# Recurrence on 28 segments of 112 steps instead of 16 of 196, handled one step at a time

## The chip, the core and the metric

The kernel runs on one core of a Trainium2 chip. A core has five engines with queues of their own: TensorE (PE in the profile; its weight loads are PEld), VectorE (DVE), ScalarE (ACT), GpSimd (POOL) and SyncE (SP), which issues the DMAs here. They are ordered only by semaphores. The metric is the device time of one execution in microseconds, lower is better.

## The reference, cut to what matters

The input is x, (16, 56, 56, 128) in float32: 16 images of T = 3136 tokens with 128 channels. Layer 0 is a shifted window attention after a group norm. Layer 1 is a causal linear attention and then this recurrence, which is where the change is:

```
t  = t + linear_attention(layernorm(t))
z  = layernorm(t) @ W.T
wx = (z - mean) * rsqrt(var + 1e-5) * gamma + beta      # over all 16*3136 tokens
for each of the 3136 tokens of an image, in order, all 16 images side by side:
    y  = sigmoid(wx[token] + y @ V.T)                   # V is orthogonal, y starts at 0
out = t + y of every token
```

## The kernel before

It has three stages, each with the work of all engines laid over one another: window attention (tiles `wa_`), linear attention (`la_`) and the recurrence (`sc_`, function `scan`).

The recurrence is made parallel by cutting each image into SEGS segments of STEPS tokens. All segments of all images run side by side as COLS = 16 x SEGS columns. Every segment but the first needs the state at the end of the one before. It gets it from a warm-up: WARM = 12 steps over the last 12 tokens of every segment, started from 0.5. Their end states are handed one segment on as start states, and then the main pass of STEPS steps runs over all tokens. After it, the true end states are compared with the start states that were used. Only if some pair differs by more than 5e-7 is the main pass run again, SEGS - 1 times.

One step t is worked in two halves h of HALF columns. TensorE issues, in `scan`'s tensor block, `state_part(t, h)` (V times the state of t-1, L1488) and `input_part(t + 1, h)` (W times the next tokens, L1478), h = 0 and then h = 1. Both accumulate in one PSUM bank of the half. In float32 each matmul stands as two instructions in the trace. ScalarE then takes the sigmoid of the half (L1562) into `sc_y`. A half's next L1488 waits for its sigmoid, so each half is a ring PE, ACT, PE, and the two halves take turns on PE.

Around it, work goes in tiles of up to LONGEST = 10 steps (`MAIN_PLAN`). SP loads a tile of tokens from DRAM scratch `t2` into `sc_tb` (4 buffers, L1436). GpSimd multiplies it by the layer-norm scale into `sc_ub` (2 buffers, L1240), two tiles ahead. VectorE transposes it in 32x32 blocks into `sc_uT` (L1503), a pair of steps at a time, three pairs ahead. It also transposes the states back: for the first 3 of 5 pairs of a tile straight into the output tile `sc_ob` (L1523), where GpSimd adds the residual in one instruction (L1463); for the others into PSUM (L1525), from where VectorE adds the residual itself (L1534). SP stores the tile (L1428). SP's queue is in order: the store of tile j-4 stands ahead of the load of tile j. GpSimd's too: the scaling of tile j stands ahead of the residual of tile j-2.

The layout ties the stages. Linear attention works in units of 256 tokens, 196 in all, one per 3.98 us, and stores each token into `t2` at segment and step; each stretch of tokens that lies in one segment is a DMA of its own (`pieces`, L789). The tail of a unit is on SP: load of unit n+4 (L780), stores of unit n-5. The blocks 0 to EARLY_BLOCKS - 1 of 32 columns are complete before the stage ends, so the first three warm-up tiles are loaded for these blocks at unit EARLY_AT (L1229), and GpSimd scales the first two of them four units later (L1240 again, among `la_spread`, `la_rstd` and `la_tn`, L1019, L1025, L1030). The remaining blocks are loaded and scaled when the stage is over. `measure_gap` (L1309) and `compare` (L1326 to L1333) come last.

Of the kernel before, what the change touches and what calls it, by code (L numbers as in the profile page):

```python
# [26 lines left out]
SEGS = 16  # L27
# [3 lines left out]
SQ = 32  # L31
# [1142 lines left out]
class Recurrence:  # L1174
# [13 lines left out]
    def allocate(self, ctx):  # L1188
        nc = self.nc

        def sb(name, shape):
# [12 lines left out]
                          ob=sb("ob", [C, KEPT_TILES, LONGEST, COLS]), uT=sb("uT", [C, U_PAIRS, 2, COLS]), y=sb("y", [C, Y_PAIRS, 2, COLS]))  # L1204
# [168 lines left out]
def scan(nc, block, t2, out, plan, ffn, signals, ident, bank):  # L1373
# [36 lines left out]
    def vector_sums(j):  # L1410

        return sum(plan[i][1] // 2 - by_pool(i) for i in range(FIRST, j))
# [57 lines left out]
    def _(pe):  # L1470
        def input_part(t, h):
# [24 lines left out]
    def _(dve):  # L1496
        def turn_tokens(p):
            if not inside(p, PAIRS):
                return
            j, i = where[p]  # L1500
            dve.wait_ge(u_made, j + 1)
            at_least(dve, w_done, 4 * (p - U_PAIRS + 1))
# [3 lines left out]
        def hand(p):  # L1506
            if p != 1 or not WARMED:
# [6 lines left out]
        def turn_states(p):  # L1514
            if not inside(p, PAIRS) or p < WARM_PAIRS:
                return
            j, i = where[p]
            for h in range(2):
                dve.wait_ge(y_made[h], 2 * p + 2)
            at_least(dve, stored[slot(j)], stores(j))  # L1520
            states = y[:, p % Y_PAIRS].rearrange("p s c -> p (s c)")
            if i < 2 * by_pool(j):
                nc.vector.transpose(ob[:, slot(j), i:i + 2, :].rearrange("p s c -> p (s c)"), states).then_inc(y_turned, 1)  # L1523
            else:
                nc.vector.transpose(b_y[p % 2], states).then_inc(y_turned, 1)  # L1525
# [106 lines left out]
```

## Time and profile before

| | us |
|---|---|
| median of 3 runs | 1782.33 |
| lowest and highest | 1781.41, 1783.42 |
| profiled execution, its own time | 1784.76 |
| profiled execution, span of instructions | 1782.8 |
| window attention | 0 to about 771 |
| linear attention | about 771 to 1568 |
| recurrence | about 1574 to 1774 |

The profiled execution is one execution under the profiler. Its own time is 1.9 us above its span, and 2.4 us above the median of the runs. Stage borders are read from where the stages' instructions start.

### The profile page before, as it was taken

To read this page: it belongs to the slowest core of one execution; us is meant where nothing else is said; L and a number is where in the kernel's file an instruction comes from. 1 tells how busy PE (TensorE), PEld (TensorE's weight loads), DVE (VectorE), ACT (ScalarE), POOL (GpSimd) and SP (SyncE) were. 2 spreads that over 40 slices of the span, in tenths; PEclk is the share of its full clock that TensorE was granted. 3 is DMA by queue.
4 is the path that set the end of the run, shared out by engine and by line. 5 is a ranking of instruction groups with operands and counts; after the bars stand their busy time and mean duration, and the time that the engine had idled before them with its cause. 6 is when DMAs were issued, how large, how long until landed. Compare 5 with 4: busy or idle time off the path is not lost.

```text
span 1782.8 us, 58142 instructions
## 1 busy us (share of the span) xinstructions
PE 1749.7 (98%) x19648; PEld 1587.7 (89%) x19648; DVE 1509.8 (85%) x4546; ACT 1269.8 (71%) x3387; POOL 1073.7 (60%) x1202
## 2 busy tenths in 40 slices
PE   7999999999999999989999999999999999989997
PEld 6888888888888888879999999999999999989997
DVE  7889888888888888778888888888888888868787
ACT  5877778887887788856666666666666666657776
POOL 6887888888888888843333333333333333368874
PEclk9999999999999999999999999999999999999999
DMA  5333343433333332313334434343434443457774
GB/s 167 105 103 104 104 110 99 109 107 102 110 103 104 106 106 70 83 43 70 73 67 68 70 68 70 68 67 68 70 68 70 68 68 70 86 178 277 291 278 176
DMA packets 361816, 188.30 MB, mean 106 GB/s; under 512 B 221760, under 2 KB 348720, under 8 KB 356656
## 3 DMA queue, kind: packets, MB, share of 16 engines
q1 hardware_dynamic: 360368, 183.40, 41.0%
q8 instruction: 164, 2.69, 0.7%
q14 instruction: 132, 1.08, 0.2%
q10 hardware_dynamic: 1152, 1.13, 0.2%
HBM read 106.58 MB, written 77.87 MB: 103 GB/s over the span
## 4 chain that ended last, share of the span: by engine, by line
PE 52%; issue 28%; POOL 17%; DVE 1%; DMA 1%; POOLq 0%; ACT 0%; ACTq 0%; SPq 0%; DVEq 0%
POOL la_rstd L1025 12%; PE k_psum L349 7%; PE k_psum L299 6%; PE k_psum L292 6%; PE k_psum L1488 6%; PE k_psum L317 6%; PE k_psum L333 6%; PE k_psum L365 5%; PE k_psum L1478 5%; PE k_psum L283 5%; POOL la_spread L1019 3%; POOL la_tn L1030 2%; DMA wa_group<-in_group 0%; POOLq L42 0%; DMA t<-la_tn 0%
## 5 line engine op out<-in xcount | busy, mean ns | idle before, releaser
L1019 POOL TENSOR_SCALAR la_spread<-la_mv 128x4 f32<-128x4 f32 (+1 forms) x203 | 46.2, 228 | 476.1 <-DVE la_mv L1130 476.0
L618 POOL TENSOR_TENSOR wa_prob<-wa_prob,wa_peak 128x784 f32<-128x784 f32 x128 | 195.0, 1523 | 116.8 <-DVE wa_peak L484 116.8
L966 ACT ACTIVATE la_ve<-k_psum 128x256 f32<-128x256 f32 x196 | 75.6, 386 | 231.9 <-PE k_psum L847 231.9
L1025 POOL TENSOR_TENSOR la_rstd<-la_spread,k_exponent 128x4 f32<-128x4 f32 (+1 forms) x203 | 207.8, 1024 | 17.2 <-POOL la_spread L1019 0.4
L625 POOL TENSOR_TENSOR wa_prob<-wa_prob,wa_inv 128x784 f32<-128x784 f32 x128 | 195.2, 1525 | 11.3 <-DVE wa_inv L445 11.3
L835 PE MATMUL k_psum<-la_uT,la_wt 128*128 128x256 f32 x784 | 201.9, 380 | 0.0
L1085 DVE SCALAR_TENSOR_TENSOR la_fqk<-k_psum,la_raised 128x512 f32<-128x512 f32 x196 | 135.4, 691 | 72.8 <-ACT la_raised L958 72.6
L1562 ACT ACTIVATE sc_y<-k_psum,sc_cols 128x128 f32<-128x128 f32 x414 | 152.3, 368 | 51.9 <-PE k_psum L1488 8.8
L476 DVE TENSOR_TENSOR wa_prob<-k_psum,wa_bias 128x784 f32<-128x784 f32 x128 | 124.9, 976 | 66.2 <-PE k_psum L317 66.1
L1488 PE MATMUL k_psum<-sc_y,sc_vT 128*128 128x128 f32 x824 | 171.0, 289 | 0.0
L958 ACT ACTIVATE la_raised<-k_psum,la_minus_one 128x512 f32<-128x512 f32 x196 | 134.8, 688 | 43.9 <-PE k_psum L835 43.7
L1478 PE MATMUL k_psum<-sc_uT,sc_fT 128*128 128x128 f32 x832 | 161.7, 276 | 2.8 <-DVE sc_uT L1503 2.8
L525 ACT ACTIVATE wa_kb<-k_psum,wa_own 128x392 f32<-128x392 f32 x256 | 136.5, 584 | 38.2 <-PE k_psum L292 38.2
L544 ACT ACTIVATE wa_vb<-k_psum 49x256 f32<-49x256 f32 x256 | 97.0, 379 | 90.8 <-PE k_psum L299 89.1
L333 PEld LDWEIGHTS k_psum<-k_ident,wa_prob 113*128 113x128 f32 x1024 | 118.2, 142 | 43.5 <-issue 23.7
L886 PE MATMUL k_psum<-la_ve,la_kt 128*128 128x129 f32 (+1 forms) x768 | 150.7, 278 | 1.8 <-ACT la_state L982 1.6
L904 PE MATMUL k_psum<-la_ve,la_aT 128*128 128x129 f32 x784 | 151.7, 276 | 0.0
L908 PE MATMUL k_psum<-la_state,la_fqk 128*128 128x129 f32 (+1 forms) x768 | 148.9, 275 | 0.0
L637 POOL TENSOR_TENSOR wa_xb<-wa_xw,wa_bout 112x384 f32<-112x384 f32 (+1 forms) x128 | 146.9, 1148 | 0.0
L349 PE MATMUL k_psum<-wa_pT,wa_vb 128*64 128x49 f32 x4096 | 146.5, 224 | 0.1
L556 ACT ACTIVATE wa_pT<-k_psum 128x452 f32<-128x452 f32 x256 | 140.2, 548 | 8.4 <-PE k_psum L333 5.3
L349 PEld LDWEIGHTS k_psum<-wa_pT,wa_vb 128*64 128x64 f32 x4096 | 130.0, 138 | 17.8 <-ACT wa_pT L556 0.5
(137 smaller groups left out, 5205.3 us busy)
## 6 DMA issues: line engine op xcount, KB each, us to landing
la_xc<-x SPq DMA_DIRECT2D x196, 128.0 KB, 3.0
wa_xT<-in_x_cm SPq DMA_DIRECT2D x124, 196.0 KB, 3.3
sc_tb<-t SPq DMA_DIRECT2D x17, 1320.0 KB, 8.3
out<-sc_ob SPq DMA_DIRECT2D x17, 1280.0 KB, 5.4
wa_xw<-in_x_tok SPq DMA_DIRECT2D x64, 224.0 KB, 2.7
wa_xw<-in_x_tok SPq DMA_DIRECT2D x64, 168.0 KB, 2.3
x<-wa_y SPq DMA_DIRECT2D x64, 168.0 KB, 2.8
x<-wa_y SPq DMA_DIRECT2D x48, 224.0 KB, 2.9
```

Source lines behind the costliest of these rows:

```text
L333: mm = nc.tensor.transpose(b_pt[:, q * LANES:(q + 1) * LANES], prob[0:LANES, k % S, hp, 2 * h + p].rearrange("p j c -> p (j c)"), ident[0: ...
L349: mm = nc.tensor.matmul(b_ot[64 * hp:64 * hp + 64, c:c + WIN], vb[:, k % S, h * 2 + w // 2, w % 2, hp].rearrange("p a b -> p (a b)"), pT[: ...
L618: nc.gpsimd.tensor_tensor(s, s, peak[:, k % S, :].unsqueeze(2).broadcast_to([128, PAIRS * HEADS, WIN]), ALU.subtract).then_inc(lowered, 1)
L625: nc.gpsimd.tensor_tensor(s, s, inv[:, k % S, :].unsqueeze(2).broadcast_to([128, PAIRS * HEADS, WIN]), ALU.mult).then_inc(weighted, 1)
L835: mm = nc.tensor.matmul(b_qk[:, j * 2 * P:(j + 1) * 2 * P], wt[:, j * C:(j + 1) * C], uT[:, n % S, :], start=True, stop=True)
L886: nc.tensor.matmul(b_kv[:, 0:E], kt[part, n % S, a, :], ve[part, n % S, a, :], start=fresh, stop=True, skip_group_check=True).then_inc(kv_ ...
L904: mm = nc.tensor.matmul(held[:, a * E:(a + 1) * E], aT[:, n % S, a, :], ve[:, n % S, a, :], start=True, stop=begins(c), skip_group_check=True)
L908: mm = nc.tensor.matmul(held[0:p, a * E:(a + 1) * E], fqk[:, n % S, 0, a * P:a * P + p], state[:, c % S, :], start=False, stop=True, skip_ ...
L1025: nc.gpsimd.tensor_tensor(rstd[:, n % S, used], spread[:, used], exponent[:, used], ALU.pow).then_inc(rooted, 1)
L1478: nc.tensor.matmul(b_state[h][t % 2][:, 0:HALF], ffn.fT[:, :], uT[:, t // 2 % U_PAIRS, t % 2, half(h)], start=True, stop=False).then_inc(w ...
L1488: nc.tensor.matmul(b_state[h][t % 2][:, 0:HALF], ffn.vT[:, :], before, start=False, stop=True).then_inc(v_done[h], 1)
L1562: nc.scalar.activation(ffn.state(t)[:, half(h)], b_state[h][t % 2][:, 0:HALF], ACT.Sigmoid, bias=ffn.shift_bn).then_inc(y_made[h], 1)
```

## The change

SEGS goes from 16 to 28, so STEPS from 196 to 112, COLS from 256 to 448, HALF from 128 to 224 and NB (blocks of 32 columns) from 8 to 14. WARM stays 12, so there are 124 steps instead of 208. A tile has at most 6 steps. VectorE takes one step of 448 columns at a time instead of a pair of 2 x 256. GpSimd adds the residual of two thirds of a tile's steps instead of three fifths. EARLY_BLOCKS is 12 of 14 instead of 7 of 8. The core of the diff:

```diff
-SEGS = 16
+SEGS = 28
 STEPS = T // SEGS
 COLS = B * SEGS
 HALF = COLS // 2
...
-MAIN_PLAN = [(0, 4, True), (4, 8, True)] + [(12 + 10 * j, 10, True) for j in range(17)] + [(182, 8, True), (190, 4, True), (194, 2, True)]
+MAIN_PLAN = [(0, 2, True), (2, 4, True)] + [(6 + 6 * j, 6, True) for j in range(16)] + [(102, 5, True), (107, 3, True), (110, 2, True)]
...
-LONGEST = 10
+LONGEST = 6
 KEPT_TILES = 3
-U_PAIRS = 4
-Y_PAIRS = 3
-EARLY_BLOCKS = 7
+U_STEPS = 5
+Y_STEPS = 5
+EARLY_BLOCKS = 12
...
     def by_pool(j):
-        return plan[j][1] // 2 * 3 // 5 if FIRST <= j < TILES - 2 else 0
+        return plan[j][1] * 2 // 3 if FIRST <= j < TILES - 2 else 0
...
-            nc.vector.transpose(uT[:, p % U_PAIRS].rearrange("p s c -> p (s c)"),
-                                ub[:, j % 2, i:i + 2].rearrange("p s b r -> p (s b r)")).then_inc(u_turned, 1)
+            nc.vector.transpose(uT[:, t % U_STEPS, :], ub[:, j % 2, i].rearrange("p b r -> p (b r)")).then_inc(u_turned, 1)
...
-                nc.vector.transpose(b_y[p % 2], states).then_inc(y_turned, 1)
+                at_least(dve, summed, vector_steps(t - 1))
+                nc.vector.transpose(b_y[t % 2][:, 0:COLS], ffn.state(t)).then_inc(y_turned, 1)
...
-        for p in range(-3, PAIRS + 1):
-            hand(p)
-            turn_states(p - 1)
+        for t in range(-4, NT + 1):
+            hand(t)
+            turn_states(t - 1)
...
-            turn_tokens(p + 3)
-            residual(p - 1)
+            turn_tokens(t + 4)
+            residual(t - 1)
```

VectorE in the middle of the recurrence, one tile before (10 steps, 5 pairs), with the semaphores that each instruction waits for:

```order
L1523 STREAM_TRANSPOSE sc_ob<-sc_y 128x512 [waits sc_stored1,sc_y_made1,sc_y_made0]
L1503 STREAM_TRANSPOSE sc_uT<-sc_ub 128x512 [waits sc_w_done,sc_u_made]
L1523 STREAM_TRANSPOSE sc_ob<-sc_y 128x512 [waits sc_stored1,sc_y_made1,sc_y_made0]
L1503 STREAM_TRANSPOSE sc_uT<-sc_ub 128x512 [waits sc_w_done,sc_u_made]
L1523 STREAM_TRANSPOSE sc_ob<-sc_y 128x512 [waits sc_stored1,sc_y_made1,sc_y_made0]
L1503 STREAM_TRANSPOSE sc_uT<-sc_ub 128x512 [waits sc_w_done,sc_u_made]
L1525 STREAM_TRANSPOSE k_psum<-sc_y 128x512 [waits sc_stored1,sc_y_made1,sc_y_made0]
L1503 STREAM_TRANSPOSE sc_uT<-sc_ub 128x512 [waits sc_w_done,sc_u_made]
L1534 TENSOR_TENSOR sc_ob<-k_psum,sc_tb 128x512 [waits sc_y_turned]
L1525 STREAM_TRANSPOSE k_psum<-sc_y 128x512 [waits sc_stored1,sc_y_made1,sc_y_made0]
L1503 STREAM_TRANSPOSE sc_uT<-sc_ub 128x512 [waits sc_w_done,sc_u_made]
L1534 TENSOR_TENSOR sc_ob<-k_psum,sc_tb 128x512 [waits sc_y_turned]
```

And the last two of four straight transposes and the first step by way of PSUM in a tile now (6 steps; `k_psum` is the bank that the transpose goes through):

```order
L1523 STREAM_TRANSPOSE sc_ob<-sc_y 128x448 [waits sc_stored0,sc_y_made1,sc_y_made0]
L1505 STREAM_TRANSPOSE sc_uT<-sc_ub 128x448 [waits sc_w_done,sc_u_made]
L1523 STREAM_TRANSPOSE sc_ob<-sc_y 128x448 [waits sc_stored0,sc_y_made1,sc_y_made0]
L1505 STREAM_TRANSPOSE sc_uT<-sc_ub 128x448 [waits sc_w_done,sc_u_made]
L1526 STREAM_TRANSPOSE k_psum<-sc_y 128x448 [waits sc_stored0,sc_summed,sc_y_made1,sc_y_made0]
L1505 STREAM_TRANSPOSE sc_uT<-sc_ub 128x448 [waits sc_w_done,sc_u_made]
L1535 TENSOR_TENSOR sc_ob<-k_psum,sc_tb 128x448 [waits sc_y_turned]
```

A tile has 14 instructions instead of 12, each over 448 elements per partition instead of 512, and the transpose through PSUM waits for `sc_summed` as well. SP's queue at the early loads, before (`la_xc` is the load of a unit, `t` the scratch `t2`):

```order
L789 DMA t<-la_tn 128x4x33
L1229 DMA sc_tb<-t 128x2x231 [waits la_stored4,la_stored5,la_stored3,la_stored6,la_stored2,la_stored7,la_stored1,la_stored0]
L1229 DMA sc_tb<-t 128x4x231
L1229 DMA sc_tb<-t 128x6x231
L780 DMA la_xc<-x 128x2x128 [waits la_attended]
L789 DMA t<-la_tn 56x4x33 [waits la_tabled]
L789 DMA t<-la_tn 72x4x33
L789 DMA t<-la_tn 124x4x33
```

and now:

```order
L789 DMA t<-la_tn 96x4x33
L1229 DMA sc_tb<-t 128x2x396 [waits la_stored4,la_stored5,la_stored3,la_stored6,la_stored2,la_stored7,la_stored1,la_stored0]
L1229 DMA sc_tb<-t 128x4x396
L1229 DMA sc_tb<-t 128x6x396
L780 DMA la_xc<-x 128x2x128 [waits la_attended]
L789 DMA t<-la_tn 16x4x33 [waits la_tabled]
L789 DMA t<-la_tn 112x4x33 x2
L789 DMA t<-la_tn 16x4x33
```

The three loads are at the same place of the queue (at unit 182 instead of 186) with 396 elements instead of 231 per row, and the stores of a unit are cut into other pieces: 784 in the whole stage instead of 640. GpSimd's scaling of the first two tiles, which stands after `la_tn` of unit 190, is now after that of unit 186 and has 2x384 and 4x384 elements instead of 2x224 and 4x224. The stores of the last two units are

```order
L789 DMA t<-la_tn 120x4x33 [waits la_tabled]
L789 DMA t<-la_tn 8x4x33
L789 DMA t<-la_tn 128x4x33
L789 DMA t<-la_tn 60x4x33 [waits la_tabled]
L789 DMA t<-la_tn 68x4x33
L789 DMA t<-la_tn 128x4x33
```

before the change, and with it

```order
L789 DMA t<-la_tn 64x4x33 [waits la_tabled]
L789 DMA t<-la_tn 64x4x33
L789 DMA t<-la_tn 48x4x33
L789 DMA t<-la_tn 80x4x33
L789 DMA t<-la_tn 32x4x33 [waits la_tabled]
L789 DMA t<-la_tn 96x4x33
L789 DMA t<-la_tn 16x4x33
L789 DMA t<-la_tn 112x4x33
```

that is, eight instead of six.

## Rows read from the trace of the kernel before

**Rows 1.** Page: chain that ended last, by engine.

```profile
PE 52%; issue 28%; POOL 17%; DVE 1%; DMA 1%; POOLq 0%; ACT 0%; ACTq 0%; SPq 0%; DVEq 0%
```

**Rows 2.** Windows of the recurrence: stretch, busy by engine, clock, DMA share, GB/s.

```profile
1574.00:1590.00 16.00, 15.44 (x118) 15.47 (x119) 6.62 (x11) 10.14 (x28) 13.06 (x5) 0.89 0.69 275
1590.00:1765.00 175.00, 175.00 (x1481) 175.00 (x1480) 141.94 (x222) 136.03 (x371) 134.47 (x38) 1.00 0.70 261
```

**Rows 3.** Timeline, one step and a later stretch: start, length, engine, line, shape, count.

```profile
1651.75 1.31 ACT L1562 ACTIVATE sc_y<-k_psum,sc_cols 128x128 f32<-128x128 f32 x3
1651.77 0.43 PE L1488 MATMUL k_psum<-sc_y,sc_vT 128*128 128x128 f32 x2
...
1652.72 0.32 PE L1488 MATMUL k_psum<-sc_y,sc_vT 128*128 128x128 f32 x1
...
1755.89 10.33 ACT L1562 ACTIVATE sc_y<-k_psum,sc_cols 128x128 f32<-128x128 f32 x22
```

**Rows 4.** Timeline, PE alone, in linear attention and just after it.

```profile
1301.78 1.03 PE L835 MATMUL k_psum<-la_uT,la_wt 128*128 128x256 f32 x4
1302.65 0.38 PE L857 MATMUL k_psum<-k_ident,la_fqk 128*128 128x128 f32 x2
...
1567.93 0.83 PE L1222 MATMUL k_psum<-k_ones 128*128 128x128 f32 x6
1568.60 0.39 PE L1300 MATMUL k_psum<-k_gram,sc_cT 128*128 128x129 f32 x2
```

**Rows 5.** Groups of 1575 to 1775 by shape: count, busy, mean ns, idle before.

```profile
L1562 ACT ACTIVATE sc_y<-k_psum,sc_cols 128x128 f32<-128x128 f32 x414 | 152.3, 368 | 51.9 <-PE k_psum L1488 8.8
...
L1240 POOL TENSOR_TENSOR sc_ub<-sc_tb 128x2560 f32<-128x2560 f32 x17 | 75.7, 4455 | 30.7 <-DVE sc_uT L1503 30.7
...
L1463 POOL TENSOR_TENSOR sc_ob<-sc_ob,sc_tb 128x1536 f32<-128x1536 f32 x17 | 54.0, 3177 | 1.2 <-DVE sc_ob L1523 1.2
```

**Rows 6.** Timeline of DVE in one tile of the recurrence.

```profile
1654.60 0.73 DVE L1525 STREAM_TRANSPOSE k_psum<-sc_y 128x512 f32<-128x512 f32 x1 [0.59 <-ACT sc_y L1562]
1655.23 0.67 DVE L1503 STREAM_TRANSPOSE sc_uT<-sc_ub 128x512 f32<-128x512 f32 x1
1655.83 0.65 DVE L1534 TENSOR_TENSOR sc_ob<-k_psum,sc_tb 128x512 f32<-128x512 f32 x1
1656.49 0.73 DVE L1525 STREAM_TRANSPOSE k_psum<-sc_y 128x512 f32<-128x512 f32 x1
```

**Rows 7.** Tile `sc_tb`: time from issue to landing of its loads.

```profile
DMA to landing us min/median/max: 1.9/8.2/9.7
```

**Rows 8.** DVE at the early loads; DMA rate of 1511 to 1545 in 40 slices.

```profile
1528.88 0.49 DVE L1118 BATCH_NORM_STATS2 la_stats<-la_xc 128x6 f32<-128x128 f32 x2 [2.01 <-DMA la_xc<-x]
...
GB/s 140 40 105 21 55 110 99 50 0 142 33 64 80 156 156 249 363 378 374 236 50 32 191 101 43 18 136 82 38 65 138 70 99 0 106 56 47 94 11 0
```

**Rows 9.** Timeline at the early scaling on POOL.

```profile
1537.83 0.60 DVE L1074 TENSOR_SCALAR la_u<-la_xc,la_mv,la_rstd 128x128 f32<-128x128 f32 x2
...
1540.37 2.58 POOL L1240 TENSOR_TENSOR sc_ub<-sc_tb 128x448 f32<-128x448 f32 x2
...
1541.81 1.48 DVE L1074 TENSOR_SCALAR la_u<-la_xc,la_mv,la_rstd 128x128 f32<-128x128 f32 x2
...
1543.50 0.57 DVE L1145 SCALAR_TENSOR_TENSOR la_tn<-k_psum,la_rden,la_xc 128x128 f32<-128x128 f32 x2
...
1544.42 0.39 PE L904 MATMUL k_psum<-la_ve,la_aT 128*128 128x129 f32 x2
```

**Rows 10.** Timeline between the stages: the last unit's stores, PE's first matmul.

```profile
1566.94 1.39 SPq L789 DMA_DIRECT2D t<-la_tn  x3
...
1574.56 0.68 PE L1478 MATMUL k_psum<-sc_uT,sc_fT 128*128 128x128 f32 x4 [2.83 <-DVE sc_uT L1503]
```

**Rows 11.** Chain of work that ended last, in its tail: start, length, what.

```profile
1774.60 0.29 DVE sc_gap L1309
...
1776.15 0.41 DVE sc_worst L1328
```

More of the change, by code:

```diff
@@ L1385, in scan @@
     TILES = len(plan)
-    where = [(j, i) for j in range(TILES) for i in range(0, plan[j][1], 2)]
-    PAIRS = len(where)
-    NT = 2 * PAIRS
+    where = [(j, i) for j in range(TILES) for i in range(plan[j][1])]
+    NT = len(where)
     FIRST = sum(not kept for _, _, kept in plan)
-    pairs_to = [sum(size for _, size, _ in plan[0:j]) // 2 for j in range(TILES + 1)]
-    WARM_PAIRS = pairs_to[FIRST]
-    WARMED = 2 * WARM_PAIRS
+    steps_to = [sum(size for _, size, _ in plan[0:j]) for j in range(TILES + 1)]
+    WARMED = steps_to[FIRST]
     def by_pool(j):
-        return plan[j][1] // 2 * 3 // 5 if FIRST <= j < TILES - 2 else 0
+        return plan[j][1] * 2 // 3 if FIRST <= j < TILES - 2 else 0
     def loads(j):
@@ L1410, in vector_sums, with vector_steps @@
     def vector_sums(j):
-        return sum(plan[i][1] // 2 - by_pool(i) for i in range(FIRST, j))
+        return sum(plan[i][1] - by_pool(i) for i in range(FIRST, j))
+    def vector_steps(t):
+        return sum(i >= by_pool(j) for j, i in where[WARMED:max(WARMED, t)])
     def slot(j):
@@ L1512, in hand, with turn_states @@
             nc.vector.memset(begins[:, :, 0:1], 0.0).then_inc(handed, 1)
-        def turn_states(p):
-            if not inside(p, PAIRS) or p < WARM_PAIRS:
+        def turn_states(t):
+            if not inside(t, NT) or t < WARMED:
                 return
-            j, i = where[p]
+            j, i = where[t]
             for h in range(2):
-                dve.wait_ge(y_made[h], 2 * p + 2)
+                dve.wait_ge(y_made[h], t + 1)
             at_least(dve, stored[slot(j)], stores(j))
-            states = y[:, p % Y_PAIRS].rearrange("p s c -> p (s c)")
-            if i < 2 * by_pool(j):
-                nc.vector.transpose(ob[:, slot(j), i:i + 2, :].rearrange("p s c -> p (s c)"), states).then_inc(y_turned, 1)
-            else:
-                nc.vector.transpose(b_y[p % 2], states).then_inc(y_turned, 1)
@@ L1527, in residual @@
-        def residual(p):
-            if not inside(p, PAIRS) or p < WARM_PAIRS:
+            if i < by_pool(j):
+                nc.vector.transpose(ob[:, slot(j), i, :], ffn.state(t)).then_inc(y_turned, 1)
+            else:
+                at_least(dve, summed, vector_steps(t - 1))
+                nc.vector.transpose(b_y[t % 2][:, 0:COLS], ffn.state(t)).then_inc(y_turned, 1)
+        def residual(t):
+            if not inside(t, NT) or t < WARMED:
                 return
-            j, i = where[p]
-            if i < 2 * by_pool(j):
+            j, i = where[t]
+            if i < by_pool(j):
```

39 lines of the change are left out of this document (19 added, 20 removed).

## The prediction

> **What bounds the kernel now.** I read the chain that ended last, then the windows of the recurrence, then the timeline of one step. The chain lies on PE for half of the span, with POOL next [rows 1]; the change touches the last 200 us and, by way of `t2`, the stage before. In the recurrence PE shows 175.00 of 175.00 us busy, at the full clock, with DVE at 81%, ACT at 78%, POOL at 77% and DMA at 0.70 [rows 2]. That looks like a stage bound by PE's work, and the timeline says that it isn't quite. Two sigmoids 104.14 us apart (1651.75 and 1755.89) are 110 steps apart (22 sigmoids in 10.33 us, 0.37 for the last, give 0.949 per step), so a step takes 0.9467 [rows 3]. PE would issue its eight instructions faster: 6 of 128 columns start in 0.67 us, 0.1117 each [rows 4], and eight make 0.894. What a step waits for is the ring of one half: matmul 1651.77 to 1652.20, sigmoid of 0.368 [rows 5], and the same half's next matmul at 1652.72 [rows 3]; 0.43 + 0.37 leaves 0.15 for three handovers. So 0.053 us of a step is latency, and the rest is PE.
>
> **The steady recurrence.** 208 steps of 0.9467 are 196.9 us. Now a step has eight PE instructions of 224 columns. Four of 256 columns start in 0.87 us, 0.2175 each [rows 4]; between 0.1117 and 0.2175, 224 columns take 0.191, and a step 1.529 us. Would the ring bind? Its matmul grows by 0.08 for the first instruction and about as much for the second, to 0.6, the sigmoid from 0.368 to at most 0.644 (in proportion, 224/128; 0.45 if most of it is fixed), with 0.15 of handovers: at most 1.4, under 1.529. PE sets the pace, and 124 steps take 189.6. **-7.3 us.** The columns passed have grown (124 x 448 against 208 x 256, by 4%), since the warm-up of 12 steps is paid on every segment; what is won is the latency and the fixed part of each instruction.
>
> The other engines must keep 9.17 us per tile of 6 steps. VectorE: at 512 elements a transpose is followed by the next after 0.63 (1654.60 to 1655.23), a token transpose by the residual after 0.60 and a residual by its follower after 0.66 [rows 6]. Six times 0.63 and 0.60 and twice 0.66 are 8.7 even if 448 elements were no shorter than 512; at 0.067 less for each it is 7.8. The two steps by way of PSUM take 1.7 against 1.53 and lag by 0.2 each; the four others (1.1) catch up, with five buffers on either side. The added wait for `sc_summed` is on residuals issued two steps earlier; behind it stand the token transpose and, four steps on, PE, so it costs nothing. GpSimd: 2688/2560 of 4.455 and 1792/1536 of 3.177 [rows 5] are 4.68 and 3.71, 8.4 of 9.17, against 7.6 of 9.47 before. It fits with 0.8 us left. Both are covered by PE; if GpSimd took 10% more, this cover would be gone.
>
> **What the layout moves in the stage before.** First the early loads. They carry 12 steps x 12 blocks instead of 12 x 7, 2.43 MB instead of 1.42, ahead of a unit's load in SP's queue. Already now VectorE waits 2.01 us for that load, and the rate in this stretch tops out at 378 GB/s [rows 8]. Another 1.01 MB at 378 are 2.7 us, which PE gets in full, as the slack is used up. Bounds: 0 (if the queues were not full) and 4.1 (at the 249 GB/s of the slice before the peak). I take **+2.7**, as the peak slices are where only these loads move.
>
> Second, the scaling of two warm-up tiles on GpSimd takes 2.58 us for 1344 elements, and VectorE's two `la_u` instructions, which need nothing from it, take 1.48 instead of 0.60: they end when it ends. After it, `la_tn` ends at 1544.07, and PE's matmul starts on time at 1544.42, 0.35 later [rows 9]. 2304 elements take 960 x 1.74 ns = 1.67 more, so VectorE is held 1.67 longer; less the 0.35, **+1.3** (0 to 1.7).
>
> The Trainium skill has this rule (SBUF — State Buffer, "SBUF: two separate sides"): GpSimd and a VectorE instruction that uses both read ports exclude each other from a shared pair of ports for a whole instruction. By that rule the trace agrees (0.60 against 1.48), and the hold grows with the GpSimd instruction in full; the 0 end of my bound would be ruled out. In the recurrence the transposes have one source, and the residual on VectorE has one of its sources in PSUM, so by it nothing is held there.
>
> Third, between the stages, stores of the last two units are 8 instead of 6, and the unit before has 4 instead of 3. Three issues take 1.39 [rows 10], so up to three more cost 1.4, and some idle time of SP is in between: **+1.2** (0 to 1.6). The late loads and the scaling of the first tile are twice as large but short; the first token transpose is shorter: **+0.1**. The 144 issues more in the whole stage lie beside 3.98 us of PE per unit and cost nothing.
>
> Clock: the stretch to 1590 was granted 0.89 of full on the mean [rows 2], so some 3.5 us at the lower level, 1.2 GHz, after PE had been idle for 2.83 us [rows 10]. A step bound by PE loses half of that, 1.75; a step with latency in it lost about 1.4. **+0.3**, between -0.3 and, if a second such stretch comes with the longer idle time, +2.
>
> **The tail.** Three comparisons and a reduction go over 432 instead of 240 elements, at 0.29 to 0.41 each now [rows 11]. In proportion they add 1.1, with a fixed part 0.6; the last matmul and sigmoid add 0.2. **+0.8** (0.4 to 1.3).
>
> **Sum.** -7.3 + 2.7 + 1.3 + 1.2 + 0.1 + 0.3 + 0.8 = -0.9. The profiled execution would take 1784.76 - 0.9 = 1783.9 (span 1781.9), and the median, which is 2.43 lower, 1781.4. That is no change: a measurement of this kernel can tell about 0.2%, 3.6 us.
>
> **Rivals.**
> 1. The give-backs are hidden. The early loads meet another unit and other stores, and VectorE has idle time in every unit before and after. Then only half of the 4.0 of the first two terms arrives and 0.6 between the stages: -0.9 - 2.6 = -3.5, and with all of it hidden -6.1. About 1777.5. For it: at the early scaling PE lost nothing so far, and I know its slack from one place only. Against it: VectorE waited 2.01 for the load with today's size.
> 2. The feed of the recurrence becomes the bound: store of tile j-2, load of tile j+2 behind it in SP's queue, its scaling and the residual behind that on GpSimd, store of tile j. With 0.5 for issues and handovers this ring takes 8.9 us plus the landing, for two tiles of 18.3 us. It decides from a landing of 9.4 us on. Landings were 8.2 in the median and 9.7 at most [rows 7]; a tile's bytes grow by 5%, and the rate from 261 to about 280 GB/s. At a landing of 10.5 a tile takes 9.7, 0.5 over, for 17 tiles 9 us, of which the tokens' lead takes about half (a tile is scaled three steps, 4.6 us, before its first transposition): 1781.4 + 4.4 = 1785.8; at 11, 1789. I put it at 1787, slower. Against it: the mean landing would have to rise by a fifth.
> 3. The change doesn't do what it says: with 27 handed states per image instead of 15 one differs by over 5e-7, and the main pass is run 27 more times, over 4 ms. Against it: a sigmoid's slope is at most 1/4 and V is orthogonal, so 12 steps shrink a difference of at most 0.5 in 128 channels (5.7 in length) by 4 to the 12th, to 3.4e-7. 1 in 100.
>
> **How the numbers follow.** The forecast has 0.55, rival 1 0.28, rival 2 0.16, rival 3 0.01. The forecast's own terms reach from about -4 to +3 around 1781.4, with most of it within 0.2%: same 0.54. Faster by over 0.2% (below 1778.8) is rival 1 and the forecast's lower edge, 0.29. Slower (above 1785.9) is most of rival 2 and the upper edge, 0.17. The range 1776.8 to 1786.8 leaves out the far end of rival 1 and the upper half of rival 2.
>
> **What would show it.** Steady sigmoids of one half 1.53 us apart, and PE's first to last matmul of the recurrence about 192 us instead of 199. A wait of VectorE for `la_xc` of 4 to 5 us near unit 185 instead of 2.01. A VectorE `la_u` pair of about 3.1 us beside the early scaling. PE's first matmul of the recurrence 5 to 6 us later than 1574.56. GpSimd at over 90% in the steady stretch, without waits of VectorE for `sc_ub`. I'd be wrong if the step is longer than 1.55 (then the ring or the feed binds), or if the recurrence starts less than 3 us later (then rival 1).

## The result and the profile after

The changed kernel takes 1792.27 us (median of 4 runs, 1790.58 to 1794.37) against 1782.12 for the kernel before in the same rounds: ratio 1.0057, 95% interval 1.0039 to 1.0074. I had forecast 1781.4 with a range up to 1786.8. It is slower, by 10 us. On another chip, later, the ratio was 1.0025 (1.0012 to 1.0038).

The profiled execution took 1792.99 us, its span is 1791.3 (before: 1784.76 and 1782.8). Cut by stages, the two spans differ like this. Each border is the start of a matmul of PE, but for the one between the last two rows, which is the end of the last input matmul.

| stretch | before | after | difference | forecast |
|---|---|---|---|---|
| start to unit 180 of linear attention | 1493.65 | 1493.09 | -0.6 | 0 |
| unit 180 to unit 195 (early loads, early scaling) | 61.19 | 71.20 | +10.0 | +4.0 |
| unit 195 to the recurrence | 19.72 | 26.22 | +6.5 | +1.3 |
| the recurrence's input matmuls, first to last | 198.10 | 189.53 | -8.6 | -7.0 |
| tail | 10.17 | 11.26 | +1.1 | +0.8 |

The recurrence gained what it should, and a bit more. Windows of the recurrence, answering to [rows 2] (busy by engine PE, PEld, DVE, ACT, POOL, then clock, DMA share, GB/s):

```profile
1590.00:1600.00 10.00, 9.49 (x38) 9.05 (x39) 5.11 (x10) 3.52 (x8) 6.92 (x3) 0.73 1.03 392
1600.00:1780.00 180.00, 180.00 (x953) 180.00 (x952) 149.53 (x265) 106.35 (x239) 149.75 (x39) 1.00 0.70 264
```

Timeline of ACT, answering to [rows 3]; the same half comes every second row:

```profile
1656.36 0.45 ACT L1562 ACTIVATE sc_y<-k_psum,sc_cols 128x224 f32<-128x224 f32 x1 [0.31 <-PE k_psum L1490]
1657.11 0.45 ACT L1562 ACTIVATE sc_y<-k_psum,sc_cols 128x224 f32<-128x224 f32 x1 [0.31 <-PE k_psum L1490]
1657.87 0.45 ACT L1562 ACTIVATE sc_y<-k_psum,sc_cols 128x224 f32<-128x224 f32 x1 [0.31 <-PE k_psum L1490]
...
1754.72 0.45 ACT L1562 ACTIVATE sc_y<-k_psum,sc_cols 128x224 f32<-128x224 f32 x1 [0.31 <-PE k_psum L1490]
```

From 1656.36 to 1754.72 are 65 steps, 1.513 us each; I had 1.529. ACT waits 0.31 for PE before every sigmoid: PE sets the pace, as forecast. The groups by shape say the same of the covers, answering to [rows 5]:

```profile
L1562 ACT ACTIVATE sc_y<-k_psum,sc_cols 128x224 f32<-128x224 f32 x237 | 106.0, 447 | 73.3 <-PE k_psum L1490 73.3
...
L1240 POOL TENSOR_TENSOR sc_ub<-sc_tb 128x2688 f32<-128x2688 f32 x16 | 74.7, 4668 | 12.3 <-DVE sc_uT L1505 6.5 <-DMA sc_tb<-t 5.8
...
L1465 POOL TENSOR_TENSOR sc_ob<-sc_ob,sc_tb 128x1792 f32<-128x1792 f32 x16 | 58.8, 3677 | 1.4 <-DVE sc_ob L1523 1.4
```

GpSimd needs 4.67 + 3.68 = 8.35 us for a tile of 9.08 (forecast 8.4). It waits 5.8 us in all for loads of `sc_tb`, and PE nothing for it. The landings were 8.4 us in the median and 11.9 at most, against 8.2 and 9.7 [rows 7].

The loss is ahead of the recurrence, in two places. First the early loads. DVE's timeline, answering to the first line of [rows 8], and SyncE's queue there:

```profile
1518.53 0.49 DVE L1118 BATCH_NORM_STATS2 la_stats<-la_xc 128x6 f32<-128x128 f32 x2 [8.82 <-DMA la_xc<-x]
```

```profile
1504.66 2.67 SPq L1229 DMA_DIRECT2D sc_tb<-t  x3
1507.37 0.93 SPq L780 DMA_DIRECT2D la_xc<-x  x1
1508.35 4.58 SPq L789 DMA_DIRECT2D t<-la_tn  x4
1512.98 0.46 SPq L780 DMA_DIRECT2D la_xc<-x  x1
```

VectorE waits 8.82 us instead of 2.01. Behind the burst four stores take SyncE 4.58 us to issue, where four took 1.78 to 3.35 in the six units before. That is not new, as the kernel before has the same row behind its smaller loads:

```profile
1524.23 4.48 SPq L789 DMA_DIRECT2D t<-la_tn  x4
```

The early scaling on POOL stands as forecast, answering to [rows 9]:

```profile
1532.31 4.17 POOL L1240 TENSOR_TENSOR sc_ub<-sc_tb 128x768 f32<-128x768 f32 x2
1533.95 2.87 DVE L1074 TENSOR_SCALAR la_u<-la_xc,la_mv,la_rstd 128x128 f32<-128x128 f32 x2
...
1537.86 0.46 PE L904 MATMUL k_psum<-la_ve,la_aT 128*128 128x129 f32 x2 [0.32 <-DVE la_tn L1145]
```

The pair `la_u` takes 2.87 instead of 1.48, 1.39 more, and the unit there was 5.36 us long instead of 3.98: +1.4, forecast +1.3.

The second place is the end of linear attention, answering to [rows 10]: SyncE's queue, then the three engines behind it.

```profile
1576.74 4.23 SPq L789 DMA_DIRECT2D t<-la_tn  x6
1587.24 1.44 SPq L1229 DMA_DIRECT2D sc_tb<-t  x3
```

```profile
1589.28 0.40 POOL L1240 TENSOR_TENSOR sc_ub<-sc_tb 128x128 f32<-128x128 f32 x1 [8.74 <-DMA sc_tb<-t]
1589.71 1.17 DVE L1505 STREAM_TRANSPOSE sc_uT<-sc_ub 128x448 f32<-128x448 f32 x2 [7.81 <-POOL sc_ub L1240]
...
1590.51 0.71 PE L1480 MATMUL k_psum<-sc_uT,sc_fT 128*128 128x224 f32 x1 [9.12 <-DVE sc_uT L1505]
```

The last store is issued by 1580.97, and the late loads, which wait until all stores have landed, at 1587.24. The chain that ended last has one row for that:

```profile
1580.54 6.51 DMA t<-la_tn
```

The wait is on the landing of stores, to whose issue I had given the whole term. In the tail the reduction takes 0.61 instead of 0.41 [rows 11] and the whole 1.1 more:

```profile
1782.11 0.49 DVE sc_gap L1309
...
1784.10 0.61 DVE sc_worst L1328
```

### The profile page after: what moved, and what is told of

The parts are those of the page before. It is cut to its first block, busy times and chain, and to the rows that moved or that the text cites. A ratio compares the mean times of both kernels' runs of the same rounds, so it can differ in the third digit from the quotient of the medians.

```text
span 1791.3 us, 56538 instructions
## 1 busy us (share of the span) xinstructions
PE 1742.9 (97%) x18976; PEld 1579.1 (88%) x18976; DVE 1511.2 (84%) x4580; ACT 1226.4 (68%) x3219; POOL 1080.3 (60%) x1200
## 4 chain that ended last, share of the span: by engine, by line
PE 52%; issue 29%; POOL 17%; DVE 1%; DMA 1%; POOLq 0%; SPq 0%; ACT 0%; ACTq 0%; DVEq 0%
POOL la_rstd L1025 11%; PE k_psum L349 8%; PE k_psum L299 6%; PE k_psum L292 6%; PE k_psum L317 6%; PE k_psum L333 5%; PE k_psum L365 5%; PE k_psum L1480 5%; PE k_psum L1490 5%; PE k_psum L283 5%; POOL la_spread L1019 3%; POOL la_tn L1030 2%; POOLq L42 0%; DMA t<-la_tn 0%; SPq L789 0%
## 5 line engine op out<-in xcount | busy, mean ns | idle before, releaser
L1562 ACT ACTIVATE sc_y<-k_psum,sc_cols 128x224 f32<-128x224 f32 x246 | 110.0, 447 | 91.8 <-PE k_psum L1490 91.8
L1480 PE MATMUL k_psum<-sc_uT,sc_fT 128*128 128x224 f32 x496 | 135.9, 357 | 9.1 <-DVE sc_uT L1505 9.1
L835 PEld LDWEIGHTS k_psum<-la_uT,la_wt 128*128 128x128 f32 x784 | 134.7, 192 | 10.2
```

What stands on the lines that cost most here:

```text
L835: mm = nc.tensor.matmul(b_qk[:, j * 2 * P:(j + 1) * 2 * P], wt[:, j * C:(j + 1) * C], uT[:, n % S, :], start=True, stop=True)
```

## The experiments

Three theories stood at the start, for both places. Theory 1: the number of stores (784 instead of 640) loads SyncE's queue. Theory 2: the row distance of `t2` (1848 B instead of 1056) makes the stores slow. Theory 3: the bytes of the early loads do it.

This table holds what the runs have in common. "Landing" is the median of `la_xc` between 900 and 1480 us, "wait" the longest of VectorE for `la_xc` at the early loads, "gap" the time from PE's first matmul of unit 195 to its first of the recurrence, and "PE" the wait for `sc_uT` in front of that one. The expectations count the gap from a later matmul of linear attention, so their numbers (3.6 for the kernel before, 9.9 for the first profile of the changed one) are 16.1 to 16.3 lower than the table's.

| run | landing | wait | gap | PE | time, and of before in that job |
|---|---|---|---|---|---|
| before (profile of the start) | 3.1 | 2.0 | 19.7 | 2.8 | |
| c0_before_again | 3.0 | 2.3 | 19.8 | 2.9 | 1781.34, 1782.80 |
| after (first profile) | 3.4 | 8.8 | 26.2 | 9.1 | 1792.27, 1782.12 |
| c1_changed_again | 2.7 | 7.1 | 23.0 | 5.9 | 1787.65, 1781.56 |
| c2_changed_timed | 3.4 | 8.6 | 25.5 | 8.3 | 1790.32, 1786.39 |
| x1_four_stores | 3.2 | 2.9 | 21.9 | 5.0 | 1785.09, 1784.39 |
| x5_padded_rows | 2.9 | 3.2 | 23.0 | 6.1 | 1785.49, 1781.56 |
| x7_padded_four | 3.0 | 3.8 | 22.9 | 6.0 | 1788.59, 1781.56 |
| x2_seven_blocks | 2.7 | 3.1 | 24.1 | 7.0 | 1779.56, 1784.39 |
| x8_ten_blocks | 2.7 | 6.6 | 23.5 | 6.4 | 1786.24, 1781.56 |
| x4_spread_early | 2.7 | 2.6 | 22.6 | 5.5 | 1781.25, 1784.39 |
| x9_two_waves | 2.7 | 2.9 | 22.8 | 5.7 | 1777.71, 1782.80 |
| x3_two_store_queues | 2.7 | 7.5 | 23.2 | 5.6 | 1787.90, 1784.39 |
| x10_last_units_narrow | 2.9 | 7.8 | 24.3 | 7.2 | 1791.50, 1782.80 |
| x11_last_units_wide | 2.9 | 7.5 | 23.0 | 5.9 | 1787.44, 1782.80 |
| x13_eight_stores | 3.4 | 9.2 | 29.5 | 12.4 | 1795.05, 1786.39 |
| x14_half_rows | 3.5 | 9.2 | 20.3 | 3.2 | 1811.55, 1786.39 |

**x1, four stores in every unit of the kernel before.**

```diff
                     token = upto
+            while len(found) < 4:
+                big = max(range(len(found)), key=lambda i: found[i][2] - found[i][1])
+                a, p, q, col, s = found[big]
+                cut = (q - p) // 2 // 16 * 16 or (q - p) // 2
+                found[big:big + 1] = [(a, p, p + cut, col, s), (a, p + cut, q, col, s + cut)]
             return found
```

> The kernel before (16 segments, its layout of t2, its early loads), with one edit: in each unit of linear attention that stores in three pieces, the largest piece is cut in two, so that all 196 units issue four stores (784 in all instead of 640). Bytes, addresses and packets of data stay. Theory 1 (each store costs the queue a fixed time of about 0.65 us until it has landed, whatever its size, so that four stores and a load fill most of a unit's 3.98 us): the steady stage stays at its pace, VectorE's wait for la_xc after the early loads grows from 2.0 to 4 to 6 us, the time from the last matmul of linear attention to the first of the recurrence grows from 3.6 to 8 to 10 us, and the whole is 6 to 9 us longer, 1788 to 1791 against 1782. Theory 2 (the new layout's token stride, 1848 B instead of 1056, makes the stores slow): both stay, 1782 to 1783. Theory 3 (only the bytes of the early loads count): the same, 1782 to 1783.

The wait grew by 0.9 and the gap by 2.1; the time, one run, was 0.7 over the kernel before. Theory 1 expected 6 to 9: at the early loads the number of stores is a small part.

**x2, seven blocks early.**

```diff
-EARLY_BLOCKS = 12
+EARLY_BLOCKS = 7
...
-        EARLY_AT = EARLY + 14
+        EARLY_AT = 182
```

> The changed kernel with 7 instead of 12 of its 14 blocks in the early loads, issued at the same unit as in the changed kernel. 1.42 MB instead of 2.43 go ahead of the unit's load, as in the kernel before; the late part grows to 7 blocks, 1.42 MB instead of 0.41. Theory 3 (bytes of the early loads): VectorE's wait for la_xc falls from 8.8 to about 2 us, and the gap between the stages grows by what the late bytes take. Theory 1 (number of stores): the early wait falls only to 4 to 5 us, since the queue is already close to full with four stores per unit; the late loads of 1.0 MB more cost 3 to 4 us in the gap, which is 13 to 14 us instead of 9.9. Theory 2 (layout): as theory 1 for the early wait. Whole: 1789 to 1793 in all of them, so the two places tell, not the sum.

The wait fell to 3.11, and the whole to 1779.56, 4.8 below the kernel before in that job, with one run of each: theory 3 at this place. I had expected 1789 to 1793 of every theory, with 3 to 4 us back in the gap; the larger late part cost 1.1.

**x3, two queues for the last stores.**

```diff
-                    store(n - 5)
+                    store(sp, n - 5, (0, 1) if n - 5 < SPLIT_FROM else (0,))
...
                     scale_tokens(n - 5)
+                    if n - 5 >= SPLIT_FROM:
+                        store(act, n - 5, (1,))
```

> The changed kernel, in which the stores of the second half (tokens 128 to 255) of the last 8 units of linear attention are issued by ScalarE on its own DMA queue instead of by SyncE. Number, size and addresses of the stores stay. Theory 1 (the stores wait for one another within one queue): the last of them lands about 2 us sooner or more, the gap between the stages falls from 9.9 to 5 to 7 us and the whole by 3 to 5 us, to 1787 to 1789. Theory 2 (each packet of a store takes long at its place in memory, because of the layout) or a backlog in the 16 DMA engines themselves: the gap stays at 9 to 10 us.

The gap stayed at 23.2, with a later run of the changed kernel (c1) at 23.0. SyncE's queue in c1, then in x3, where ScalarE's last store is issued by 1575.21:

```profile
1559.44 19.94 SPq L789 DMA_DIRECT2D t<-la_tn  x27
1581.70 1.44 SPq L1229 DMA_DIRECT2D sc_tb<-t  x3
```

```profile
1559.22 16.19 SPq L771 DMA_DIRECT2D t<-la_tn  x13
1581.74 1.44 SPq L1234 DMA_DIRECT2D sc_tb<-t  x3
```

All stores were issued 4.0 us sooner, and the late loads, which wait until the stores have landed, went out at the same time. Here SyncE's issues are not the limit, and the stores don't wait for one another within its queue; this part of theory 1 fell.

**x4, the early loads in six portions.**

```diff
-                    if n == EARLY_AT:
+                    if n == EARLY_AT - 2:
                         stored_through(EARLY)
-                        for j in range(len(WARM_PLAN)):
-                            ffn.load_early(sp, ffn.tiles, signals, j)
+                    if EARLY_AT - 2 <= n < EARLY_AT - 2 + sum(EARLY_PARTS):
+                        j, part = [(j, i) for j in range(3) for i in range(EARLY_PARTS[j])][n - EARLY_AT + 2]
+                        ffn.load_early(sp, ffn.tiles, signals, j, part)
```

> The changed kernel, with its three early loads (12 blocks) cut by blocks into six DMAs of 0.2 to 0.5 MB, one per unit, from two units earlier on (tile 0 whole, tile 1 in two, tile 2 in three parts). Bytes stay. Theory 1 (the queue is close to full in every unit, so what is put into it comes out as a wait): VectorE's waits for la_xc at this place fall from 8.8 us, but their sum stays at 3 to 6 us, spread over several units; whole 1788 to 1790. Theory 3 (a burst alone hurts: the prefetch of four units hides what comes in small portions): the waits vanish, 8 us are back, and the whole is 1784 to 1785.

1781.25, below both forecasts. Units 180 to 195 took 63.98 us instead of 70.38 (c1), with the same bytes and at the full granted clock throughout. VectorE's waits there sum to 7.3 but are 2.6 at most, and most of that is hidden: the prefetch bears small portions and not a burst.

**c1, the changed kernel again; x5, x7, wider rows in the kernel before; x8, ten blocks.** The edit of x5 (x7 has that of x1 as well), and that of x8:

```diff
+ROW = 14
-    t2 = nc.dram_tensor("t2", (C, STEPS, NB, SF), F32, kind="Internal").ap()
+    t2 = nc.dram_tensor("t2", (C, STEPS, ROW, SF), F32, kind="Internal").ap()
...
-                                      [[NB * SF, q - p], [SQ * STEPS * NB * SF, QUADS], [1, SF]])
+                                      [[ROW * SF, q - p], [SQ * STEPS * ROW * SF, QUADS], [1, SF]])
```

```diff
-EARLY_BLOCKS = 12
+EARLY_BLOCKS = 10
```

> The changed kernel as it is, once more, as the measure for the others on one chip. If what differed between chips was small: early loss of TensorE (the unit pitches over 4.32 us at the early loads) 9 us, gap between the stages 9 to 10 us, whole 8 to 10 us over the kernel before. If the changed kernel's own profile came from a chip with slower stores, the gap here is 6 to 8 us.

> The kernel before, with only the distance between two steps' rows in t2 made that of the changed kernel (14 blocks of 33 numbers, 1848 B, of which 8 are used, instead of 1056 B). Number and size of the stores stay; the loads of t2 carry the same bytes in pieces of 1056 B instead of whole runs of steps. If the layout makes the stores slow: the gap between the stages grows from 3.6 us to 6 or more and the steady stores land later. If it is the number of stores or the bytes of the loads: gap 3.6 to 4, whole within 2 us of before.

> The kernel before with both: rows of 1848 B and four stores in every unit. With the layout and the number of stores of the changed kernel but the early and late loads of the kernel before. If these two make the gap of the changed kernel: 8 to 10 us instead of 3.6. With the number alone (four stores without the padding had 2.1 us more): 5 to 6 us. At the early loads 1 us more than before in either case.

> The changed kernel with 10 of 14 blocks in the early loads (2.03 MB), at the same unit. At 7 blocks (1.42 MB) TensorE lost 1.9 us there and at 12 (2.43 MB) 9.35 us. If the burst simply lasts longer at the rate it had (about 190 GB/s from first issue to last landing, so 3.2 us for 0.61 MB) beyond a slack that is used up at 7: 1.9 + 3.2 = 5 us. If SyncE's blocking on a full queue adds to it in proportion: 6.4 us. If it is a cliff between 10 and 12: 2 to 3 us. GpSimd's hold on VectorE at unit 188 comes to 0.5 to 0.9 us (1.05 at 12 blocks, 0 at 7).

c1 lost 8.6 at units 184 and 185, but its gap is 23.0, not 26.2: 3 us of the first profile's gap go with a slower condition, seen as 3.4 against 2.7 in the landings of the whole stage. What makes the condition, no run shows. Wider rows alone took the gap to 23.0, and with four stores to 22.9: the two don't add up. Together they have the whole gap of the changed kernel in its quicker condition, though counted as in the expectation it is 6.7, below the 8 to 10 that I had given. At the early loads they cost VectorE up to 1.8 us.

x8: units 180 to 195 took 69.31, against 62.35 for seven blocks and 70.38 for twelve. Without the hold at unit 188 (0.7 of x8's, 1.4 of c1's), the first 0.61 MB more cost TensorE 6.2 us and the next 0.40 MB 0.4. At units 184 and 185 TensorE lost 8.1 in x8, more than any of the three forecasts. No line through the bytes gives that; it looks like a step between seven and ten. c1 and x2 are the pair to read it from, since their queues begin within 0.01 us of each other. DVE in c1, then in x2:

```profile
1515.38 0.49 DVE L1118 BATCH_NORM_STATS2 la_stats<-la_xc 128x6 f32<-128x128 f32 x2 [7.14 <-DMA la_xc<-x]
```

```profile
1511.35 0.49 DVE L1118 BATCH_NORM_STATS2 la_stats<-la_xc 128x6 f32<-128x128 f32 x2 [3.11 <-DMA la_xc<-x]
```

SyncE's queue in c1, then in x2:

```profile
1503.18 2.04 SPq L1229 DMA_DIRECT2D sc_tb<-t  x3
1505.26 0.99 SPq L780 DMA_DIRECT2D la_xc<-x  x1
1506.30 4.25 SPq L789 DMA_DIRECT2D t<-la_tn  x4
1510.59 1.19 SPq L780 DMA_DIRECT2D la_xc<-x  x1
```

```profile
1503.19 1.87 SPq L1229 DMA_DIRECT2D sc_tb<-t  x3
1505.10 0.55 SPq L780 DMA_DIRECT2D la_xc<-x  x1
1505.70 3.05 SPq L789 DMA_DIRECT2D t<-la_tn  x4
1508.79 0.43 SPq L780 DMA_DIRECT2D la_xc<-x  x1
```

And the windows of these 12 us (columns as in the windows above) in c1, then in x2:

```profile
1503.00:1506.00 3.00, 3.00 (x26) 2.85 (x25) 2.62 (x13) 2.51 (x8) 1.46 (x3) 1.00 0.58 74
1506.00:1509.00 3.00, 3.00 (x26) 2.85 (x25) 2.06 (x13) 1.64 (x6) 1.42 (x3) 1.00 0.99 342
1509.00:1512.00 3.00, 2.23 (x21) 2.04 (x19) 0.00 (x0) 1.82 (x7) 0.04 (x1) 1.00 1.05 389
1512.00:1515.00 3.00, 0.00 (x0) 0.00 (x0) 0.00 (x0) 0.40 (x2) 0.00 (x0) 1.00 0.90 186
```

```profile
1506.00:1509.00 3.00, 3.00 (x26) 2.85 (x25) 2.06 (x13) 1.64 (x6) 1.41 (x3) 1.00 1.00 331
1509.00:1512.00 3.00, 2.25 (x21) 2.05 (x19) 0.65 (x4) 1.82 (x7) 0.04 (x1) 1.00 1.14 247
1512.00:1515.00 3.00, 2.13 (x15) 1.98 (x16) 2.97 (x16) 0.93 (x3) 0.94 (x2) 1.00 0.25 28
```

The rate I used is there (342 and 389 GB/s). Yet the load behind the burst is awaited until 4.03 us later, not 2.7: when most of the burst's bytes are through, the window from 1512 still holds its last packets, the load and small packets of stores, at 186 GB/s. The second load is issued later too, at 1510.59 instead of 1508.79, but that costs nothing: VectorE comes to it 3.3 us after the first one, in both runs, and doesn't wait.

The rest is TensorE's clock. PE in c1, then in x2, at the first matmul behind the wait:

```profile
1516.90 1.22 PE L870 MATMUL k_psum<-la_fqk 128*128 128x128 f32 x4 [5.66 <-DVE la_fqk L1085]
```

```profile
1512.87 0.71 PE L870 MATMUL k_psum<-la_fqk 128*128 128x128 f32 x4 [1.62 <-DVE la_fqk L1085]
```

And the windows of the next unit, from its first matmul to that of the one after it, in c1, then in x2:

```profile
1517.91:1524.44 6.53, 6.53 (x34) 5.82 (x34) 3.93 (x19) 1.81 (x5) 1.87 (x5) 0.66 0.21 41
```

```profile
1513.41:1517.79 4.38, 4.38 (x35) 3.98 (x34) 4.25 (x23) 1.74 (x5) 1.87 (x5) 1.00 0.35 50
```

After 5.66 us without work PE runs at the lower level, 1.2 GHz, for a while: 0.66 on the mean over 6.53 us is 4.3 us of work at the full clock, which is what the unit takes in x2. That is 2.2 us in this unit, and 0.47 from the matmul above to the end of its own unit (1.01 instead of 0.54). First unit +4.5, second +2.2, together 6.7 for 1.01 MB: 4.0 of wait and 2.6 of clock. x8 has the same: PE idle for 5.13, then a unit of 6.61 at a granted clock of 0.65. So 2.7 of the 6.2 us between seven and ten blocks are the clock. The rest is the wait, 3.1, 6.6 and 7.1 us for seven, ten and twelve blocks, and why that is uneven isn't settled.

**c0, x9, x10, x11.** c0 is the kernel before. The waves of x9:

```diff
+WAVES = [(130, 10, 0, 6), (182, 1, 6, 12)]
...
-                    if n == EARLY_AT:
-                        stored_through(EARLY)
-                        for j in range(len(WARM_PLAN)):
-                            ffn.load_early(sp, ffn.tiles, signals, j)
+                    for at, apart, low, high in WAVES:
+                        if n == at:
+                            stored_through(-(-high * SQ * STEPS // (2 * P)))
+                        for j in range(len(WARM_PLAN)):
+                            if n == at + j * apart:
+                                ffn.load_early(sp, ffn.tiles, signals, j, slice(low, high))
```

> The kernel before as it is, for its trace on the same chip as the next ones. If the differences of single traces at the end of the linear attention are real: last unit's first matmul to the recurrence's first matmul 19.7 us within 0.5, VectorE's wait at the early loads costs TensorE 0.7 us. If single traces scatter by the 3.2 us by which two traces of the changed kernel differ there: anywhere from 19.7 to 23.

> The changed kernel with its early loads in two waves: blocks 0 to 5 of the three tiles at units 130, 140 and 150, long before they are needed, and blocks 6 to 11 at units 182, 183 and 184, one tile per unit; GpSimd's early scaling is cut in the same way into four instructions, each in an iteration of its own. Bytes and late part stay. If the burst is what costs 9 us at units 184 and 185 and the long scaling 1.0 at 188: nearly all of it comes back, at most 1 to 1.5 us are left (1.2 MB in portions of 0.2, 0.4 and 0.6 MB), and the whole is 8 to 9 us less than the changed kernel, and 2 to 4 us less than the kernel before (ratio 0.998 to 0.999), since the recurrence's 8.5 us remain and the gap keeps 3 us. If the bytes cost the same wherever they go in (queue full in every unit): the whole is at least 1786 and not below the kernel before.

x9 takes 1777.71 us (6 runs, 1776.81 to 1779.65) against 1782.80: ratio 0.9972, interval 0.9960 to 0.9984. That is 5.1 less than the kernel before, more than the 2 to 4 that I had expected. Units 180 to 195 take 61.67 us, where the kernel before takes 61.44 (c0) and the changed one 70.38 (c1), and the granted clock stays at 1.00 there: of the 8.7 us, 2.6 are clock that is no longer lost. What is left of the burst is one wait, after the third portion:

```profile
1514.82 0.49 DVE L1121 BATCH_NORM_STATS2 la_stats<-la_xc 128x6 f32<-128x128 f32 x2 [2.88 <-DMA la_xc<-x]
```

The scaling of six blocks of one tile takes 1.47 us, and the unit that was 5.36 long is short again: a cut hold is hidden.

The pair on row distance at the end differs in the blocks per row of the scratch tensor, 8 in x10 and 14 in x11, in its declaration and in the first line here. Both leave out the results of the last tokens:

```diff
+                        where, row = (t2[0], NB) if n < UNITS - 10 else (t2[1], 8)
...
+                    if n >= 40 and n < 104 and n % 4 == 0:
+                        s = (n - 40) // 4 * 7
+                        sp.dma_start(t2[0][:, s:s + 7, NB - 1, :], ones[:, 0:SF].unsqueeze(1).broadcast_to([128, 7, SF])).then_inc(filled, 16)
```

> The changed kernel, in which the last ten units of linear attention store into a scratch tensor whose rows are 1056 B apart (as in the kernel before) instead of 1848 B; number and size of stores stay. Their part of t2 is filled earlier with ones by 16 small DMAs, so the results of the last tokens are left out. To be read against the next one. If the distance of the rows makes the stores slow: last unit to recurrence falls from 23 to 20 to 21 us. If it is the number of stores: it stays at 23.

> The same as the one before it, but with the scratch tensor's rows 1848 B apart, as in the changed kernel. Both theories: last unit to recurrence 23 us, as in the changed kernel. It is the measure for the run with narrow rows.

Narrow rows have the longer gap, 24.3 against 23.0. So the pair gives no sign that the distance of the rows slows the stores. It isn't a clean test, since the four parts of a token come closer too, from 6.6 to 3.8 MB apart. They lie 6.6 MB apart in the kernel before and in the changed one, and 11.6 in x5. What made x5 slow is left open.

**c2, x13, x14: number or rows.** x13 cuts every piece of the last ten units in two, x14 keeps only its first half:

```diff
+            if n >= UNITS - 10:
+                found = [(a, low, high, col, s + low - p) for a, p, q, col, s in found
+                         for low, high in ((p, (p + q) // 2), ((p + q) // 2, q))]
```

```diff
+            if n >= UNITS - 10:
+                found = [(a, p, (p + q) // 2, col, s) for a, p, q, col, s in found]
```

> The changed kernel as it is, timed in rounds against the kernel before on another chip. 6 to 10 us more than the kernel before (ratio 1.003 to 1.006). Last unit to recurrence 23 us, or 26 if this chip takes the stores as slowly as the first one did.

> The changed kernel with every store of the last ten units cut in two (8 instead of 4 per unit, same rows and bytes). If each store costs a fixed 0.3 to 0.65 us beside its rows: the last ones land 5 us or more later and last unit to recurrence is 28 us or more, against 23. If only rows count: 23 to 25, the rest being SyncE's issues (0.45 us each, 8 for the last unit instead of 4, 1.8 us).

> The changed kernel with each store of the last ten units cut to its first half of the rows (number stays at 4 per unit, bytes are halved; the other tokens' t2 is filled earlier with ones, so their results are left out). If rows count: last unit to recurrence 20 to 21 us. If the number counts: 22.5 to 23.5.

All three ran on one chip in the slower condition. c2 came out 3.9 us over the kernel before and not 6 to 10; the median of the kernel before was 1786.39 in this job, and 1781.56 to 1784.39 in the others. Half the rows take the gap from 25.5 to 20.3, nearly that of the kernel before; twice the number takes it to 29.5, which lies between my two forecasts (+5 or more, and up to +2). SyncE's queue at the end, in x13, x14 and c2 in this order:

```profile
1569.19 17.72 SPq L792 DMA_DIRECT2D t<-la_tn  x38
1588.83 1.44 SPq L1232 DMA_DIRECT2D sc_tb<-t  x3
```

```profile
1598.34 4.89 SPq L793 DMA_DIRECT2D t<-la_tn  x12
1606.01 1.44 SPq L1238 DMA_DIRECT2D sc_tb<-t  x3
```

```profile
1572.00 7.21 SPq L789 DMA_DIRECT2D t<-la_tn  x11
1584.04 1.44 SPq L1229 DMA_DIRECT2D sc_tb<-t  x3
```

In c2 the late loads go out 4.8 us after the last store has been issued, in x14 2.8, in x13 1.9. So in x13 SyncE's issues are the limit (38 without a pause, 0.47 each), and in the changed kernel it is the landing of the rows, as x3 showed. Stores hurt in two ways: rows take their time until they have landed, and issues take SyncE's. But both kernels store the same 1024 rows in a unit, so the rows are not what the change made worse.

## Why the prediction was wrong

**The recurrence: right.** The step was 1.513 us for a forecast of 1.529, the other engines kept pace, and the stretch gained 8.6 where I had 7.0 with the clock term.

**The early loads: the step that failed.** "Another 1.01 MB at 378 are 2.7 us, which PE gets in full", with 4.1 as the upper bound, against 8.6 measured in the first pair of profiles. (Units 184 and 185 are 9.4 longer; the kernel before loses 0.7 of that for its own early loads, at unit 188.) In like condition, c1 against c0, it is 8.6 less 1.0, so 7.6, and x2 shows where it went. The rate was right. The load behind the burst came 4.0 later and not 2.7, near my upper bound. The clock, which I had counted only behind the stage, took 2.6: with the longer wait PE stood idle for 5.66 us and then ran at the lower level. And what I had called the same (stores, layout, place in the stage) already took VectorE's wait for seven blocks from 2.3 to 3.1, and units 180 to 195 from 61.4 to 62.4, 0.9 more. The three make 7.6. In the first pair the wait was 8.8 instead of 7.1, in the slower condition, and the clock took 1.8.

**The early scaling: right**, +1.4 for +1.3, with some luck: the pair was held 1.39 longer and not 1.67, and PE lost all of it where I had taken off 0.35. The rule that I had weighed (the Trainium skill, SBUF — State Buffer, "SBUF: two separate sides") is borne out by 2.87 against 0.60 for the same pair of instructions.

**Between the stages: the step that failed second.** I had counted issues, three at 0.46, and +1.2. Measured +3.2 (c1 against c0), and +6.5 in the first pair, whose second trace met the slower condition. I had read [rows 10] as a row of issues, but the last store's landing sets the late loads: x3 issued everything 4.0 us sooner and won nothing, x14 with half the rows won 5.2. Of what the change itself added, the number of stores is worth 2.1 by x1, in the kernel before. For the other 1.1 no run isolates the cause.

**The tail: right**, 1.1 for 0.8. **Clock:** the first 10 us of the recurrence were granted 0.73 (0.72 in c1 and x9), after PE had been idle for 9.12 us (5.9 and 5.7), so some 5.5 us at the lower level instead of 3.5. As an estimate, half of the 2 us more is 1.0 on top of the forecast's +0.3, under its upper bound of +2; no run separates it. The lower clock within linear attention, 2.6 in c1, was in no term.

Rival 1, the hidden give-backs, was the wrong way round at both places. The condition that I gave for it (recurrence later by less than 3 us) is far from the 15.95 measured. Rival 2, the feed, had landings of 8.4 and up to 11.9, but a median under the 9.4 from which it decides, and no step lengthened. The change did what it says.

Sum in like condition (c1 against c0): units 180 to 195 +8.9, gap +3.2, recurrence -8.2, tail +0.8, together +4.7. The spans differ by 6.6; the other 1.9 lie before the first unit of linear attention, where the kernels are alike. The first profile has 3 us more in the gap, in the slower condition.

## What to carry to other kernels

A bulk transfer put into a queue that feeds a pipeline costs more than its bytes over the peak rate: add the wait to the one that is there already, ask how long TensorE then stands idle, and count what it loses at the lower clock afterwards. The remedy was no smaller transfer but the same bytes in portions and earlier; it turned a loss of 0.25 to 0.6% into a gain of 0.28% (0.16 to 0.40). At a border that waits for all stores, count from the landing of the last one, not from its issue.

## What the runs showed of the hardware that was not expected

- A wait of PE inside a stage can cost more than itself. In c1 it was idle for 5.66 us, and the next unit took 6.53 us at a granted clock of 0.66; in x2 it was idle for 1.62, and the unit took 4.37 at 1.00.
- The same kernel meets two conditions: 128 KB loads land in 2.7 us in some traces and in 3.4 in others, and the gap between the stages follows (23.0 against 25.5 and 26.2). One chip number showed both, in different jobs. All traces of the kernel before and its variants show 2.9 to 3.2, so how its gap would be in the slower condition isn't known.
- Storing 132 B rows leaves the DMA engines little used while the landings run late: in c2 between 1577 and 1584 the share is 0.15 at 19 GB/s, and all wait for the last landing. A low DMA share is no sign that stores are done.

```profile
1577.00:1584.00 7.00, 1.67 (x14) 1.29 (x12) 1.47 (x7) 0.00 (x0) 0.55 (x1) 0.91 0.15 19
```

- The 16 small fillings (118 KB each, in 132 B rows) that x10, x11 and x14 have in common lengthened linear attention up to unit 180 by 1.7 to 2.6 us over c1 in the first two, and by 25.7 over c2 in the third, which met the slower condition.
